# Inverse row sums turned on VectorE and spread by DMAs, with POOL's work and the last softmax reordered, in a post-LN transformer block

## The reference

```python
qkv = einsum('bsd,ed->bse', x, w_qkv) + b_qkv            # 16 heads of 32
scores = einsum('bhqd,bhkd->bhqk', q, k) / sqrt(32) + causal
out = einsum('bhqk,bhkd->bhqd', softmax(scores), v)
x = layernorm(x + einsum('bsd,ed->bse', out, w_out) + b_out)
g, u = x @ Wg.T, x @ Wu.T                                # W = (int - 128) * scale, 2048 x 512
x = layernorm(x + (silu(g) * u) @ Wd.T)
```

## Time and profile before

| | |
|---|---|
| median of 3 runs | 739.49 us (738.57 to 745.54) |
| the profiled execution | 738.95 us, span 737.0 us |
| granted TensorE clock, mean | 0.993 |
| PE busy | 713.1 us, 97% |
| DVE, ACT, POOL busy | 390.2, 373.7, 182.1 us |
| transposes of the inverses on PE | 64, four a group |
| attention | to 378.97 us, then the FFN |

### The profile page before, as it was taken

One profiled execution on the slowest core, in us unless ns is written; L12 is line 12 of the kernel. 1 busy time (PEld: TensorE's weight loads), 2 busy tenths in 40 slices (PEclk: granted clock), 3 DMA queues, 4 the chain that ended last, 5 costly groups with the idle time before them and its releaser, 6 DMA issues.

```text
span 737.0 us, 11734 instructions
## 1 busy us (share of the span) xinstructions
PE 713.1 (97%) x4368; PEld 552.3 (75%) x4368; DVE 390.2 (53%) x992; ACT 373.7 (51%) x900; POOL 182.1 (25%) x194
## 2 busy tenths in 40 slices
PE   7999899999999999999899999999999999999994
PEld 5776676677777777776578888888888888888883
DVE  4766766566666666677543232453334532544336
ACT  3676676667866776777656555322232222322230
POOL 0011310437122660416655242221020001000004
PEclk9999999999999999999999999999999999999998
DMA  9811553336741567314498964872331003000111
GB/s 305 231 66 29 80 146 119 86 95 119 219 144 58 117 171 223 81 41 115 106 217 162 199 161 143 183 217 85 136 66 57 0 35 136 0 1 1 57 58 59
DMA packets 97207, 83.35 MB, mean 113 GB/s; under 512 B 64128, under 2 KB 73344, under 8 KB 97024
## 3 DMA queue, kind: packets, MB, share of 16 engines
q1 hardware_dynamic: 90624, 62.69, 30.6%
q0 software_dynamic: 6528, 19.93, 12.7%
HBM read 59.53 MB, written 22.02 MB: 111 GB/s over the span
## 4 chain that ended last, share of the span: by engine, by line
PE 90%; POOL 3%; ACT 2%; DVE 2%; DMA 1%; issue 0%; SPq 0%; POOLq 0%; DVEq 0%
PE bank L1508 16%; PE bank L1509 16%; PE bank L1297 12%; PE bank L1376 9%; PE bank L1516 7%; PE bank L1515 7%; PE bank L1315 6%; PE bank L1359 6%; PE bank L1397 5%; PE bank L1334 4%; ACT probs L846 1%; DVE probs L1054 1%; PE bank L1408 1%; PE bank L1263 1%; DMA x_tok<-in_L_attn_x_dram 1%; POOL scan_buf L737 1%
## 5 line engine op out<-in xcount | busy, mean ns | idle before, releaser
L846 ACT ACTIVATE probs<-probs,neg_max 128x128 f32<-128x128 f32 (+3 forms) x256 | 140.4, 552 | 3.9 <-DVE neg_max L1054 3.9
L1054 DVE CUSTOM_DVE_ANT_0 probs<-bank,causal 128x128 f32<-128x128 f32 (+3 forms) x256 | 111.7, 484 | 40.2 <-PE bank L1359 40.0
L1170 DVE SCALAR_TENSOR_TENSOR hid<-bank,u_scale,silu 128x512 f32<-128x512 f32 x64 | 48.1, 751 | 157.5 <-PE bank L1509 156.3
L1508 PE MATMUL bank<-xT_hi,gateT 128*128 128x512 f32 x256 | 99.7, 389 | 0.0
L1509 PE MATMUL bank<-xT_lo,gateT 128*128 128x512 f32 x256 | 99.6, 389 | 0.0
L1508 PE MATMUL bank<-xT_hi,upT 128*128 128x512 f32 x256 | 99.6, 389 | 0.0
L1509 PE MATMUL bank<-xT_lo,upT 128*128 128x512 f32 x256 | 99.6, 389 | 0.0
L1376 PEld LDWEIGHTS bank<-ident,probs 128*128 128x128 f32 x640 | 72.1, 142 | 34.0 <-issue 24.7
L948 ACT ACTIVATE silu<-bank,g_scale 128x512 f32<-128x512 f32 x64 | 44.0, 687 | 102.2 <-PE bank L1509 102.2
L898 ACT ACTIVATE probsT<-bank 128x512 f32<-128x512 f32 x80 | 47.7, 596 | 94.9 <-PE bank L1376 93.2
L954 ACT ACTIVATE hid_hi<-hid 128x512 fp32r<-128x512 f32 x58 | 36.7, 632 | 108.6 <-DVE hid L1170 108.6
(11 more groups left out here) (106 smaller groups left out, 1159.9 us busy)
## 6 DMA issues: line engine op xcount, KB each, us to landing
halves<-x_tok SPq DMA_DIRECT2D x7, 1024.0 KB, 6.2
x_tok<-halves SPq DMA_DIRECT2D x7, 1024.0 KB, 7.9
scan_buf<-in_L_ffn_gate_w_dram SPq DMA_DIRECT2D x4, 1024.0 KB, 6.0
scan_buf<-in_L_ffn_up_w_dram SPq DMA_DIRECT2D x4, 1024.0 KB, 5.5
scan_buf<-in_L_ffn_down_w_dram SPq DMA_DIRECT2D x4, 1024.0 KB, 5.5
w_int<-in_L_ffn_gate_w_dram POOLq DMA_DIRECT2D x16, 256.0 KB, 3.7
w_int<-in_L_ffn_up_w_dram POOLq DMA_DIRECT2D x16, 256.0 KB, 3.2
w_int<-in_L_ffn_down_w_dram POOLq DMA_DIRECT2D x16, 256.0 KB, 3.8
```

Of the source, the lines that this page charges most:

```text
L846: nc.scalar.activation(probs[qb][:, j, :], probs[qb][:, j, :], ACT.Exp, bias=neg_max[:, qb, j:j + 1], scale=-1.0, accum_out=row_sum[:, qb, ...
L1054: nc.vector.tensor_tensor_reduce(out=probs[qb][:, j, :], in0=score[j][:, first:first + w], in1=causal[:, S - w:S], scale=-SCALE, scalar=-F ...
L1170: nc.vector.scalar_tensor_tensor(out=hid[:, i % 2, :], in0=bank[:, :], scalar=u_scale[:, i:i + 1], in1=silu[:, i % 2, :], op0=ALU.mult, op ...
L1508: nc.tensor.matmul(acc[n][:, :], w[:, c, cols], form(xT_hi[:, c, :]), start=c == 0, stop=False)
```

## The change

The inverses no longer pass through PE, POOL and ACT. DVE writes the reciprocals in a row of 32 per partition (4 heads x 8 places, of which 4 are used), and turn_inverse transposes that in 32x32 blocks. store_inverse writes the result to DRAM as 4 rows of 512 tokens and more, and load_inverse reads each row back to the 32 partitions of its head (inv_rows). Both are issued by SyncE at the places that spread_inverse has in its program, for the last group by ACT at steps 8 and 10. normalise moves from step 1 to step 5, att_hi from step 2 to 6. next_lo for batch 1 moves from DVE to POOL. Weight tiles move to steps 4 and 6. Group 15's third block of scores, with its maxima and exponentials, moves from group 14's end to the start of group 15, and group 14's output products come in its first eight steps. POOL's add_bias(3) is done in groups 14 and 15 ahead of the end, and all four apply_norm in group 14.

```diff
-    INVERSE_STEP = 15
+    STORE_STEP, SPREAD_STEP = 8, 10
-    X_FIRST = [3, 5, 6, 7]
+    X_FIRST = [3, 4, 5, 6]
-    W_STEPS = {(0, 4): 8, (0, 7): 9, (1, 4): 10, (1, 7): 11, (3, 5): 12, (3, 13): 13, (4, 5): 14, (4, 13): 15}
+    W_STEPS = {(0, 4): 8, (0, 7): 9, (1, 4): 10, (1, 7): 11, (3, 4): 12, (3, 6): 13, (4, 4): 14, (4, 6): 15}
-        return (before + ahead, AMONG_X) if b < LAST else (before, [4, 4, 0, 4, 0, 4, 2, 0, 2, 0, 2, 0, 2, 0, 0, 0])
+        return (before + ahead, AMONG_X) if b < LAST else (before, AMONG_X[:8] + [0] * (STEPS - 8))
...
+        def store_inverse(eng, G):
+            eng.wait_ge(inv_turned_done, G + 1)
+            eng.dma_start(inv_dram.rearrange("j (q a r) -> (j q) a r", a=P // TURN, r=TURN).rearrange("c a r -> a c r"),
+                          inv_turned[:, :]).then_inc(inv_stored, 16)
+
+        def load_inverse(eng, G):
+            eng.wait_ge(inv_stored, 16 * (G + 1))
+            if G > 0:
+                eng.wait_ge(normed, G)
+            eng.dma_start(inv_rows[:, :], inv_dram[:, 0:S].unsqueeze(1).broadcast_to((HG, HD, S))).then_inc(inv_spread, 16)
...
+            def spread_inverse(G):
+
+                store_inverse(sp, G)
+                load_inverse(sp, G)
...
-                if G in SCAN_GROUPS[1:]:
+                if G in SCAN_GROUPS[1:] and g != 3:
                     load_scan(SCAN_GROUPS.index(G))
...
                 if g == 2:
+                    spread_inverse(G)
+                    if G + 1 in SCAN_GROUPS:
+                        load_scan(SCAN_GROUPS.index(G + 1))
                     turn(b + 2)
...
                 if g == 3:
                     store_halves(b + 2)
+                if g != 2 and G < GROUPS - 1:
+                    spread_inverse(G)
...
                 if g == 2:
                     join(b + 1)
-                    if b > 0:
-                        next_lo(b + 1, 0)
-                        next_lo(b + 1, 1)
+                    next_lo(b + 1, 0)
+                    next_lo(b + 1, 1)
                 if G > 0:
                     att_lo(G - 1)
-                if g == 2 and b > 0:
+                if g == 2:
                     next_lo(b + 1, 2)
                     next_lo(b + 1, 3)
+                    if b == LAST:
+                        add_bias(LAST, range(QH))
                 if G == GROUPS - 1:
-                    apply_norm(LAST - 1, 2)
-                    apply_norm(LAST - 1, 3)
+                    add_bias(LAST, range(QH, NT))
                     store_third()
                     choose_path()
-                widen_inverse(G)
...
-                    if s == 2 and G > 0:
+                    if s == 6 and 0 < G < GROUPS - 1:
                         att_hi(G - 1)
+                    if s == STORE_STEP and G == GROUPS - 1:
+                        store_inverse(act, G)
+                    if s == SPREAD_STEP and G == GROUPS - 1:
+                        load_inverse(act, G)
...
+            def turn_inverse(G):
+                if G > 0:
+                    dve.wait_ge(inv_stored, 16 * G)
+                wait_alone(dve, inv_done, 2 * (G + 1))
+                nc.vector.transpose(inv_turned[:, :], inv_sum[:, :, :].rearrange("p j q -> p (j q)")).then_inc(inv_turned_done, 1)
 
             def normalise(G):
 
-                wait_drained(dve, "r", G)
+                dve.wait_ge(inv_spread, 16 * (G + 1))
+                if G > 0:
+                    dve.wait_ge(att_ready, G)
                 dve.wait_ge(pv_full, G + 1)
...
+                    if s == 0 and G == GROUPS - 1:
+                        for j in range(HG):
+                            tile_max(G, 2, j)
+                        normalise(G - 1)
...
-                    if s == 1 and G > 0:
+                    if s == 5 and 0 < G < GROUPS - 1:
                         normalise(G - 1)
                     if s == 2:
                         inverse_sum(G, 0)
-                    if s == 9:
+                    if s == (8 if G < GROUPS - 1 else 5):
                         inverse_sum(G, 1)
-                    for c in x_at(G, s) if b == 0 else ():
-                        next_lo(1, c)
+                        turn_inverse(G)
```

More of the change, by code:

```diff
@@ L406, in postln_block_kernel @@
         inv_done = sem("inv_done")
-        inv_widened = sem("inv_widened")
+        inv_turned_done = sem("inv_turned_done")
+        inv_stored = sem("inv_stored")
+        inv_spread = sem("inv_spread")
         pv_full = sem("pv_full")
@@ L724, in next_lo, with add_bias @@
                                         ALU.subtract).then_inc(xT_done, 1)
[L726 to L732, removed]
+            def add_bias(b, tiles=range(NT)):
                 pool.wait_ge(bias_o_loaded, 16)
                 pool.wait_ge(z_loaded, b * 16 + 16)
-                for t in range(NT):
+                for t in tiles:
                     last = nc.gpsimd.tensor_tensor(residual(b)[:, t, :], residual(b)[:, t, :], bias_o[:, :], ALU.add)
-                last.then_inc(res_ready, 1)
+                    if t == NT - 1:
+                        last.then_inc(res_ready, 1)
             def shorten(n):
@@ L783, in _ @@
                 if g == 2 and b > 0:
-                    for t in range(NT if b < LAST else 2):
+                    for t in range(NT):
                         apply_norm(b - 1, t)
@@ L787, in _ @@
                     add_bias(b - 1)
-            add_bias(LAST)
             att_lo(GROUPS - 1)
@@ L891, in _ @@
                         next_hi(b + 1, c)
+                    if s == 0 and G == GROUPS - 1:
+                        exponential(G, 2, 0)
+                        exponential(G, 2, 1)
+                        att_hi(G - 1)
+                        exponential(G, 2, 2)
+                        exponential(G, 2, 3)
                     if exponentials_at(G, s):
@@ L1156, in _ @@
                             output_statistics(*job[1:])
-                    if g == 2 and s == (13 if b == LAST else 9) and b > 0:
+                    if g == 2 and s == 9 and b > 0:
                         variance(b - 1, mv_done, var_done)
@@ L1401, in weighted_values @@
                     last.then_inc(pv_full, 1)
-            def transpose_inverse(G):
-                acc = bank_for("r", G)
-                pe.wait_ge(inv_widened, G + 1)
-                for qb in range(NT):
-                    last = nc.tensor.transpose(acc[:, qb * P:(qb + 1) * P],
-                                               inv_wide[:, qb, :, :].rearrange("p j d -> p (j d)"), ident[:, :])
-                last.then_inc(full_of("r", G), 1)
             transpose_x(0)
@@ L1437, in _ @@
                 for s in range(STEPS):
+                    if s == 0 and G == GROUPS - 1:
+                        scores(G, (2,))
                     for m in products_at(STEPS) if s == 0 and G > 0 else ():
@@ L1455, in _ @@
                         transpose_weights(W_STEPS[G, s])
-                    if s == INVERSE_STEP:
-                        last_products = products_at(STEPS) if G == GROUPS - 1 else []
-                        for m in last_products[:-1]:
-                            weighted_values(G, m)
-                        transpose_inverse(G)
-                        for m in last_products[-1:]:
+                    if s == STEPS - 1 and G == GROUPS - 1:
+                        for m in products_at(STEPS):
                             weighted_values(G, m)
```

34 lines of the change are left out of this document (9 added, 25 removed).

## The result

| | before | after |
|---|---|---|
| median of the runs | 739.03 us (738.24 to 745.54) | 751.71 us (745.92 to 753.1) |
| ratio, 95% interval | | 1.0149 (1.0121 to 1.0176) |
| profiled execution: time, span | 738.95, 737.0 us | 745.92, 744.1 us |

The change makes the kernel 1.5% slower. The forecast was 741.3 us, with its own range 737 to 747: the sign was right and the size too small; 751.71 lies just past the upper end (751) of the whole range, in the place of rival B.

The account below looks back on a forecast made before the run. It took PE as the bound inside attention groups and SyncE's queue ahead of the FFN as the second. Gains of 5.0, 2.3 and 0.3 against +9.9 gave +2.3, 741.3 us; own range 737 to 747, 8 in 10 730 to 751.

Parts of the forecast that it names:

- rival B: In groups 8 and 12 the inverse's rows land late behind 2 MB, 5 us a group, 751 us in all; chance 14%.
- Step 1: The 64 inverse transposes leave PE: 0.355 us a group in groups 0 to 13, a gain of 5.0 us.
- Step 2: Groups 3 and 4: the bank stall behind w_lo goes as weight tiles move, 1.13 us each, a gain of 2.3 us.
- Step 3: Group 2: with next_lo on POOL, PE's hole changes its owner; gain 0.3 us, bounds -1.5 and +1.6.
- Step 4: The inverse's new path through DVE and DMA in ordinary groups: cost 0, bound 3 us each for groups 8 and 12.
- Step 5: SyncE's queue ahead of the FFN: turn(5) starts 13 us later behind group 14's spread, making the FFN +9.9 us.
- Step 6: Groups 14 and 15: attention ends 4.5 us sooner, worth 0; the last spread, 4 to 8 us after step 5, is hidden.
- PE's idling of over 8 us: Sign that the forecast is right: PE idle for over 8 us before the first down product.
- The sum: -7.6 us by the start of group 14, +9.9 us after it, together +2.3 us.

Follow-up runs that it names:

- the weight steps alone: Kernel before with only the four weight transposes of groups 3 and 4 at steps 4 and 6 instead of 5 and 13: 736.28 us.
- the late turn: Kernel before, with SyncE in group 14 waiting for that group's reciprocals before it issues turn(5): 748.19 us.
- the change again: The changed kernel run again with no edit: 750.6 us, ratio 1.0150 against the kernel before.
- the turn first: The changed kernel with turn(5) ahead of the spread of group 14's inverse rows on SyncE: 746.34 us.
- normalisation at step 4: The changed kernel with normalise at step 4, ahead of the output statistics, instead of step 5: 747.04 us.
- the rows ahead of the residual: The changed kernel with the inverse rows of groups 7 and 11 stored and loaded right after the y1 stores, ahead of the residual load: 744.94 us.
- early last rows: The changed kernel with turn(5) ahead of group 14's rows, and the last group's rows stored and loaded at ACT's steps 2 and 3: 747.61 us.
- four repairs: The changed kernel with turn(5) first, normalisation at step 4, rows of groups 7 and 11 ahead of the residual, last rows at ACT's steps 2 and 3: 738.87 us.
- the last experiment: The changed kernel with all four repairs and scales on GpSimd, plus the halves' load after the second set of transposed weight loads: 735.11 us.

## Why the prediction was right in sign and short in size

**Step 1** held: 0.41 to 0.45 us a group in groups 7, 8 and 11, which have no other wait, 0.40 by the experiment, 0.355 forecast.

**Step 2** held: 1.17 each by experiment, 1.13 forecast.

**Step 3** held in kind; its gain of 0.3 can't be told: group 2 lasted 23.65 and 22.99 us in two executions (before, and before with the weight steps alone) whose code is the same up to there, 23.00 in a third (the late turn), and 22.94 after.

**Step 4** is the step that failed, in two places. "I take 0.2, hidden, as DVE idles before its maxima" priced the turn (0.21 us measured) and looked at who waits for the rows, but not at what normalise itself stands behind at its new place. PE's products of step 8 wait for it: 0.8 us, at a price of 0.87 us a group (22.24 less 21.37), in five groups ahead of group 14 of the profiled execution, about 4.3 us, and 3.6 us by experiment (747.04 against 750.6). The second place is "It just fits: cost 0" for groups 8 and 12. The landing of y1 was put at 194, and in the profiled execution it is 194.6; in four other profiles with the same order (the change again among them) it is 195.0, 197.4, 199.6 and 199.7, so the load of the rows is issued at 204 to 209. In three of these five profiles (the change again, the turn first, normalisation at step 4) group 8 then lasts 4.7 to 7.7 us longer, group 12 at most 1. It is rival B with one group in place of two, not in every execution, and worth 5.7 us by experiment. A sum whose margin was 0.2 us on DVE, behind three transfers of which each differs by several us from one execution to the next, should have had B as its likeliest case.

The Trainium skill's rule that I cited there (DMA: Bandwidth & Descriptors, Queues, rings and completion order) points the right way: the 16 KB store took 6.0 to 8.0 us behind 2 MB and 2.0 us in the quiet hour of group 14. Of the 4.7 us that lie between the two executions shown above, though, only 1.9 are this landing; 2.8 are a later issue, behind SyncE's wait for y1.

**Step 5** held in mechanism and size: turn 13.2 later against 13, the first down product 7.2 against 7.3, tile 4's gate products 9.2 against 9.9, the whole behind group 14 9.3 against 9.9. In two other profiles with the same end it was 9.0 (the change again) and 11.5 (the rows ahead of the residual). The queue is not alone in it. The experiment with the turn first takes 4.3 us off the median (5.2 without its longest run), since the end of the attention, next in line, is then exposed; with both repaired, in the one profile of the kernel with early last rows, 1.4 of the 9.3 us are left (404.9 against 403.5). So either delay alone would have cost a large part of the 9.3. The late turn in the kernel before costs 9.7.

**Step 6** was wrong, and its error was covered by the queue of step 5: that the size behind group 14 came out right says nothing for step 6. The sign that failed with it is PE's idling of over 8 us ahead of the first down product: it was 2.5 us, as the attention ended so late. "Attention would end 4.5 us sooner": from group 14's start it ended 4.5 us later (49.9 us instead of 45.4). The last spread wasn't 4 to 8 us but 15, turned at 360.3 and used at 375.5. Stored and loaded at ACT's steps 2 and 3 the end of the attention comes 44.0 to 46.2 us after group 14's start in the five kernels that have it, 50.9 in the one with the turn first alone.

**The sum** with what was measured: -7.6 forecast for the front becomes -2.2, for the waiting products of step 8 (4.3) and small differences; +9.3 behind it; +7.1 for the short execution, and 5 to 6 us of rival B for the others: +12 to 13, as measured (12.7). The moves of next_lo to POOL, of add_bias, and of group 15's third block of scores were not tried by themselves.

## What to carry to other kernels

When an instruction is moved to a later place on its engine, look for everyone who waits for its end, the reuse of the bank that it reads included, and put in what stands ahead of it at the new place in each kind of group. A store and a load that an engine's queue has to wait for cost that queue both landings, and everything behind them, so they go behind what has a due time and ahead of what has none. Where a sum "just fits" behind the landings of large transfers, the shortest landing of one trace is not the one to build on; and a gain ahead of a queue-bound stage is only paid out when each hold of that queue is gone: here moving the scales alone gave nothing, and moving the halves' load as well 3.8 us against the kernel without either.

## What the runs showed of the hardware that I had not expected

- The landing of the same four 256 KB stores in the same place of the program differs much between executions: 2.5, 4.6 and 7.1 us in the median of the four, and SyncE's wait for them 2.8 to 7.5 us, in the five profiles with the change's order.
- The last 1 MB store of the halves landed in 5.8 us (before) and 8.8 us (four repairs) with SyncE's scales behind it, and in 15.7, 12.7 and 12.7 us in the three kernels whose scales were issued from GpSimd's queue. Why was not tried.
- Four transposed loads take 5.0 to 5.2 us of SyncE's queue at their quickest, and 11.2 us beside the 1 MB store and the scales (the last experiment).
- A transpose of 128x32 float32 in 32x32 blocks takes DVE 0.21 us.
